# Deformable-convolution stage of a four-layer MetaFormer kernel: tap-group products added up by accumulating DMAs, four product buffers, reductions three halves later

## The chip, the cores and the metric

One core of a Trainium2 chip runs one program. The metric is the device time of one execution in microseconds. The five engines run their own instruction queues and meet only at semaphores: TensorE (PE), VectorE (DVE), ScalarE (ACT), GpSimd (POOL) and SyncE (SP, here only loads and stores). PEld is TensorE's weight load.

## The reference, cut to what matters

A batch of 8 images, 32 channels, 16x16 pixels in float32, passes four layers. Each is a convolution-like mixer and a mixture-of-experts block, both with a normalisation before and a residual after. The change lies in the mixer of layer 2, a deformable convolution (DCNv4) that is applied twice in a row:

```
value  = t @ Wv + bv                       # 4 groups of 8 channels
om     = t @ Wom + bom                     # offsets and masks: 9 taps x 4 groups x 3 per pixel
loc    = pixel + tap + offset              # a real position per pixel, tap and group
out    = sum over taps( bilinear(value, loc) * mask ) @ Wo
x      = batchnorm(out), relu after the first of the two passes
```

The kernel writes the bilinear sample as two hat functions, max(0, 1 - |dx|) over the columns of the image and max(0, 1 - |dy|) times the mask over its rows. The column part is a matrix product, the row part an elementwise product, and the sum runs over rows and taps together.

## The kernel before, in words

One application is a *turn* (`deform(turn)` on each engine); there are two. A turn has 8 images `b`, each in two *halves* of 128 pixels, so 16 halves `h`. A pixel has a partition. The 9 taps of a half are three groups `t` of three taps. For each group:

- PE, `products`: 6 matrix products (hats of the columns `HX` against the values `VB`) into one of two pairs of PSUM banks, alternating by group. The group waits until the one before last has been read (`prod_used`).
- DVE, `sample` (L852): multiplies the 864 PSUM columns by the row hats `HY` and writes them to `PRD`, at the place of group `t` in the buffer of the half. Column order is point group (2), channel (16), tap and row (27).

The sum over 3 groups x 27 columns is then split. POOL's `pairs` (L294) adds group 0 to group 1 (864 columns). POOL's `last` (L301) adds the first half (432 columns) of group 2 to that sum. DVE's `sums` (L864) reduces 27 columns to one for the first 16 channels, and 2 x 27 to one for the other 16, whose group 2 is still apart, into `SMT`. `PRD` has two buffers, one for each half of an image, so `sample` waits for the `sums` and `last` of two halves before.

DVE's order, fixed in the code (L887 to L900), is: two samples, the sums of the half before, the third sample. After b = 1 five instructions (`points`) prepare images 4 to 7. POOL's order is: row distances of the next image (`rows_off`, 2 instructions), `pairs`, `last` of half 0, masks of the next image (`masked`, 2 instructions), `pairs`, `last` of half 1. PE's order interleaves, per image, six groups of products with one transpose of the next image's points (`turn_points`) and three `spread`s (3 matrix products each, which copy the column positions to 128 partitions). ACT turns the spread positions into hats: `points_out` (L499), then three times `hats` (three Abs at L515, one Relu at L518), and `rows_hat` (L505, L507) for the rows.

After the 16 halves PE runs 22 filler products (`keep_warm`), waits for all sums (`smp_ready`), and a chain of short steps on all engines does the projection and the batch normalisation before the next turn or the next layer.

`wb` holds the weights of the layers before; its 6137 columns are not read any more when a turn starts.

Of the kernel before, what the change touches and what calls it, by code (L numbers as in the profile page):

```python
# [11 lines left out]
B, C, HH, WW = 8, 32, 16, 16  # L12
NPIX = HH * WW
P = 128
B4 = P // C
# [6 lines left out]
G, CG, K9 = 4, 8, 9  # L22
NA, NR = 2, 9
GP = G // 2
PADW = HH + 2
KG = K9 * G
COLS = 2 * CG * NR
HYN = KG * NR
TRIO = 3 * GP * COLS
PRN = 3 * TRIO  # L30
HXN = K9 * NPIX
LXW = 96
BIG = 1e30
# [54 lines left out]
def metaformer(nc, x_in, cst_in, wa_in, wb_in, wc_in, wd_in, out):  # L88
    fp32 = mybir.dt.float32
    ALU, ACT, AX = mybir.AluOpType, mybir.ActivationFunctionType, mybir.AxisListType  # L90

    with ExitStack() as ctx:
        widths = {}

        def sb(name, cols, parts=P):
            t = ctx.enter_context(nc.sbuf_tensor(name, [parts, cols], fp32))
            widths[name] = cols
            return t

        def view(t, col, dims, p0=0, n=P):  # L100

            if isinstance(t, tuple):
                t, first = t
                col = first + col
            if isinstance(t, Bank):
                t, col = psum, t.at + col
            w = t.shape[1]
            return bass.AP(t, p0 * w + col, [[w, n]] + [list(d) for d in dims])

        sem = lambda name: ctx.enter_context(nc.semaphore(name))  # L110
# [4 lines left out]
        cst, wa, wb, wc, wd = sb("cst", NCST), sb("wa", NWA), sb("wb", NWB), sb("wc", NWC), sb("wd", NWD)  # L115
# [33 lines left out]

        HX, LXT, XW = (RINGS, 0), (RINGS, 2 * HXN), (RINGS, 2 * HXN + NPIX)  # L150
        HY = sb("HY", 2 * 2 * HYN)
        PRD = sb("PRD", 2 * PRN)
        SMT = sb("SMT", F)
        KC, YV = (PRD, 0), (PRD, F)

        psum = ctx.enter_context(nc.psum_tensor("bank", [P, 8 * 512], fp32))
# [60 lines left out]
        def pointed(turn, b):  # L217
# [3 lines left out]
        t_done, lxt_ready, sel_done, abs_done, hat_ready, dy_ready, hy_abs, hy_ready, hym_ready, prod_done, prod_used = (  # L221
            sem(n) for n in ("t_done", "lxt_ready", "sel_done", "abs_done", "hat_ready", "dy_ready", "hy_abs", "hy_ready",
                             "hym_ready", "prod_done", "prod_used"))
        paired = sem("paired")
        smp_ready, smp_turned, sc_ready, mean_done, mean_ready, sum_ready, sum_done, cen_ready, sq_ready, sq_done, bn_ready, dc_ready = (
            sem(n) for n in ("smp_ready", "smp_turned", "sc_ready", "mean_done", "mean_ready", "sum_ready", "sum_done", "cen_ready",
                             "sq_ready", "sq_done", "bn_ready", "dc_ready"))
# [5 lines left out]
        def after(eng, s, value):  # L233

            if not isinstance(value, int) or value > 0:
                eng.wait_ge(s, value)
# [20 lines left out]
        def _(pool):  # L257
# [33 lines left out]
                    ins = pool.tensor_tensor(hy, hy, by_point(MM, 2 * b + half), ALU.mult)  # L291
                ins.then_inc(hym_ready, 1)

            def pairs(turn, b, half):  # L294

                i = B * turn + b
                pool.wait_ge(prod_used, 6 * i + 3 * half + 2)
                first, second = (view(PRD, half * PRN + t * TRIO, [[1, TRIO]]) for t in range(2))
                pool.tensor_tensor(second, second, first, ALU.add).then_inc(paired, 1)  # L299

            def last(turn, b, half):  # L301

                i = B * turn + b
                pool.wait_ge(prod_used, 6 * i + 3 * half + 3)
                pool.wait_ge(paired, 4 * i + 2 * half + 1)
                second, third = (view(PRD, half * PRN + t * TRIO, [[1, TRIO // GP]]) for t in (1, 2))
                pool.tensor_tensor(second, second, third, ALU.add).then_inc(paired, 1)  # L307

            def top2(turn):
# [42 lines left out]
            for turn in range(2):  # L352
                rows_off(turn, 0)
                masked(turn, 0)
                for b in range(B):
                    if b + 1 < B:
                        rows_off(turn, b + 1)
                    pairs(turn, b, 0)
                    last(turn, b, 0)
                    if b + 1 < B:  # L360
                        masked(turn, b + 1)
                    pairs(turn, b, 1)
                    last(turn, b, 1)
            pool.wait_ge(prod_done, 2 * B * 6)
            pool.memset(view(VM, 0, [[1, HEADS * F]]), 0.0).then_inc(km_clear, 1)
            top2(1)
# [5 lines left out]
        def _(act):  # L372
# [136 lines left out]
            def hats(i, t):  # L509

                after(act, prod_done, 6 * (i - 1))
                hx = i % 2 * HXN + 3 * t * NPIX
                for quad in range(3):
# [79 lines left out]
        def _(dve):  # L593
# [257 lines left out]

            def sample(i, half, t):  # L852

                q = 6 * i + 3 * half + t
                dve.wait_ge(hym_ready, i + 1)
                after(dve, smp_ready, 2 * i + half - 1)
                after(dve, paired, 4 * i + 2 * half - 2)
                dve.wait_ge(prod_done, q + 1)
                dve.tensor_tensor(view(PRD, half * PRN + t * TRIO, [[3 * COLS, GP], [6 * NR, CG], [1, 6 * NR]]),  # L859
                                  view(bank[q % 2 * 2], 0, [[512, GP], [6 * NR, CG], [1, 6 * NR]]),  # L860
                                  view(HY, (i % 2 * 2 + half) * HYN + t * 3 * G * NR, [[6 * NR, GP], [0, CG], [1, 6 * NR]]),
                                  ALU.mult).then_inc(prod_used, 1)

            def sums(i, half):  # L864

                bh, b4 = divmod(i % B, B4)
                at = bh * NPIX + half * P + b4 * C
                dve.wait_ge(prod_used, 6 * i + 3 * half + 3)
                dve.wait_ge(paired, 4 * i + 2 * half + 2)
                dve.tensor_reduce(view(SMT, at, [[1, C // 2]]),  # L870
                                  view(PRD, half * PRN + TRIO, [[3 * NR, C // 2], [1, 3 * NR]]), AX.X, ALU.add)
                dve.tensor_reduce(view(SMT, at + C // 2, [[1, C // 2]]),  # L872
                                  view(PRD, half * PRN + TRIO + TRIO // GP, [[3 * NR, C // 2], [TRIO, 2], [1, 3 * NR]]), AX.XY,
                                  ALU.add).then_inc(smp_ready, 1)

            def deform(turn):
                offsets(turn, 0, 0)
                offsets(turn, 0, 1)
                points(0, 1)
                if turn == 0:  # L880
                    dve.wait_ge(vb_clear, 2)
                values(turn, 0)
                values(turn, 1)
                offsets(turn, 1, 0)
                offsets(turn, 1, 1)
                points(1, B4 - 1)
                for b in range(B):  # L887
                    i = B * turn + b
                    sample(i, 0, 0)
                    sample(i, 0, 1)  # L890
                    if b:
                        sums(i - 1, 1)
                    sample(i, 0, 2)
                    sample(i, 1, 0)
                    sample(i, 1, 1)
                    sums(i, 0)
                    if b == 1:
                        points(B4, B4)
                    sample(i, 1, 2)
                sums(B * turn + B - 1, 1)  # L900

                dve.wait_ge(sum_done, turn + 1)
                dve.tensor_copy(c1[:, 1:2], bank[2][:, 0:1]).then_inc(sum_ready, 1)
                dve.wait_ge(mean_done, turn + 1)
                dve.tensor_scalar(c1[:, 0:1], bank[3][:, 0:1], -1.0, None, ALU.mult).then_inc(mean_ready, 1)
                dve.wait_ge(sq_ready, turn + 1)
                dve.tensor_scalar(ACC[:, :], bank[1][:, :], c1[:, 0:1], None, ALU.add).then_inc(cen_ready, 1)
                dve.wait_ge(cen_ready, turn + 1)
                dve.wait_ge(sq_done, turn + 1)
                dve.tensor_scalar(c2[:, 2:3], bank[4][:, 0:1], 1e-5, None, ALU.add).then_inc(bnv_ready, 1)  # L910
                dve.wait_ge(bsd_ready, turn + 1)
                link(dve.reciprocal(c1[:, 3:4], c2[:, 1:2]))
                dve.tensor_tensor(c1[:, 2:3], c1[:, 3:4], wc[:, WC["gamma"]:WC["gamma"] + 1], ALU.mult).then_inc(bn_ready, 1)
                dve.wait_ge(bn_ready, turn + 1)
# [52 lines left out]
            for bh in range(NBH):  # L967
                for j in range(2):
                    at = (2 * bh + j) * P
# [15 lines left out]
        def _(pe):  # L985
# [240 lines left out]
            def products(turn, b, half, t):  # L1226
# [9 lines left out]
                for k3 in range(3):  # L1236
                    for gp in range(GP):
                        ins = pe.matmul(view(bank[q % 2 * 2 + gp], k3 * NR, [[3 * NR, 2 * CG], [1, NR]]),  # L1238
                                        view(HX, b % 2 * HXN + (3 * t + k3) * NPIX + half * P, [[1, P]], 64 * gp, 64),
                                        view(VB, b * COLS, [[NR, 2 * CG], [1, NR]], 64 * gp, 64),  # L1240
# [3 lines left out]
            def deform(turn, src):  # L1244
# [40 lines left out]
                pe.wait_ge(smp_ready, 16 * turn + 16)  # L1285
                turn4(bank[0], SMT, smp_turned)
                pe.wait_ge(sc_ready, turn + 1)
# [252 lines left out]
```

## Time and profile before

| | us |
|---|---|
| median of 3 runs (lowest, highest) | 507.6 (506.81, 508.44) |
| the profiled execution | 508.54 |
| span of its trace, first to last instruction | 506.7 |
| PE busy | 428.1 (84%) |
| DVE busy | 386.3 (76%) |
| ACT busy | 298.2 (59%) |
| POOL busy | 179.5 (35%) |

Busy time is the time in which the engine runs an instruction. The granted TensorE clock was 0.931 of full speed over the span. Positions in the text, such as 280.3 us, are counted from the span's start. The first turn's first sample is at 192.2 us and its last sum ends at 280.3 us; the second turn's last sum ends at 389.8 us.

### The profile page before, as it was taken

What the parts mean: (1) busy time and instruction counts of PE and PEld (TensorE: products, weight loads), DVE (VectorE), ACT (ScalarE), POOL (GpSimd) and SP (SyncE); (2) the same over time, 40 slices, a digit from 0 to 9 for tenths busy, and PEclk for the clock granted to TensorE, in tenths of its full rate; (3) what the DMA queues carried; (4) which work ended last, traced back from release to release, by engine and by line L of the source; (5) the groups of instructions that cost most, each with busy time, mean ns of one, the idle gap of its engine ahead of it and who ended that gap; (6) DMA issues with size and microseconds to landing.
All of it is one profiled execution on the core that took longest, in us unless ns stands there. A gap on an engine that the chain in (4) does not pass through costs nothing.

```text
span 506.7 us, 10694 instructions
## 1 busy us (share of the span) xinstructions
PE 428.1 (84%) x3942; PEld 294.2 (58%) x3942; DVE 386.3 (76%) x838; ACT 298.2 (59%) x634; POOL 179.5 (35%) x169
## 2 busy tenths in 40 slices
PE   6989889999988767878887879688878899699685
PEld 6868723333327645656566656566667888455474
DVE  4878899998956286789998565988996686899541
ACT  2743248888944248768880277677860323898440
POOL 5002470000000024769997045788985041000000
PEclk9999989999999598879999966988998999999995
DMA  8800000000000000000000000000000000000000
GB/s 329 352 1 1 1 0 2 1 0 1 1 0 1 1 2 1 2 2 0 3 1 1 1 2 1 1 1 1 2 3 0 1 1 1 1 2 2 1 1 21
DMA packets 1486, 9.51 MB, mean 19 GB/s; under 512 B 160, under 2 KB 928, under 8 KB 1056
## 3 DMA queue, kind: packets, MB, share of 16 engines
q1 hardware_dynamic: 1296, 8.81, 4.3%
q8 instruction: 31, 0.51, 0.4%
q14 instruction: 15, 0.12, 0.1%
q10 hardware_dynamic: 144, 0.07, 0.1%
HBM read 8.62 MB, written 0.26 MB: 18 GB/s over the span
## 4 chain that ended last, share of the span: by engine, by line
PE 53%; DVE 25%; ACT 13%; issue 6%; POOL 2%; DMA 0%; DVEq 0%; SPq 0%; POOLq 0%
PE bank L1238 13%; PE bank L1180 13%; PE bank L994 5%; PE bank L1223 4%; DVE SMT L872 4%; ACT RINGS L515 3%; DVE PRD L859 3%; ACT RINGS L566 3%; DVE RINGS L791 2%; PE bank L1345 2%; PE bank L1185 2%; DVE SMT L870 2%; PE bank L1325 2%; PE bank L1250 1%; POOL PR L314 1%
## 5 line engine op out<-in xcount | busy, mean ns | idle before, releaser
L1238 PE MATMUL bank<-VB,RINGS 64*128 64x144 f32 x1152 | 107.4, 330 | 25.2 <-DVE PRD L859 24.2
L859 DVE TENSOR_TENSOR PRD<-bank,HY 128x864 f32<-128x864 f32 x96 | 99.0, 1052 | 29.5 <-PE bank L1238 28.2
L1238 PEld LDWEIGHTS bank<-VB,RINGS 64*128 64x128 f32 x1152 | 88.4, 213 | 50.8 <-DVE PRD L859 23.6
L791 DVE TENSOR_SCALAR RINGS<-XP,wb 128x512 f32<-128x512 f32 x176 | 79.4, 527 | 7.9 <-PE bank L1180 6.6
L478 ACT ACTIVATE RINGS<-XP,wb 128x512 f32<-128x512 f32 x112 | 70.0, 714 | 17.0 <-PE bank L1180 16.9
L994 PE MATMUL bank<-cst 128*128 128x128 f32 x650 | 79.7, 283 | 0.0
L994 PEld LDWEIGHTS bank<-cst 128*128 128x128 f32 x650 | 78.3, 200 | 0.7 <-issue 0.3
L1180 PE MATMUL bank<-RINGS,cst 128*32 128x512 f32 x576 | 74.6, 600 | 3.5 <-DVE RINGS L791 3.4
L515 ACT ACTIVATE RINGS<-bank,cst 128x256 f32<-128x256 f32 x144 | 57.5, 469 | 26.4 <-PE bank L1223 26.4
L299 POOL TENSOR_TENSOR PRD<-PRD 128x864 f32<-128x864 f32 x32 | 64.7, 2022 | 17.6 <-DVE PRD L859 17.4
L282 POOL TENSOR_TENSOR HY<-OM,cst 128x324 f32<-128x324 f32 x32 | 23.3, 751 | 127.6 <-DVE LXA L841 127.6
L1180 PEld LDWEIGHTS bank<-RINGS,cst 128*32 128x32 f32 x576 | 22.9, 110 | 53.5 <-issue 26.6
L1223 PE MATMUL bank<-RINGS,cst 32*128 32x256 f32 x288 | 38.3, 475 | 10.8 <-ACT RINGS L515 6.7
L518 ACT ACTIVATE RINGS<-RINGS,cst 128x768 f32<-128x768 f32 x48 | 44.9, 936 | 1.6
L307 POOL TENSOR_TENSOR PRD<-PRD 128x432 f32<-128x432 f32 x32 | 35.3, 1103 | 16.7 <-DVE PRD L859 16.6
L384 ACT ACTIVATE sd<-var,cst 128x8 f32<-128x8 f32 x16 | 4.8, 301 | 50.4 <-DVE var L618 50.2
L314 POOL TENSOR_TENSOR PR<-PR 128x256 f32<-128x256 f32 x16 | 11.5, 729 | 63.7 <-DVE PR L703 63.7
L872 DVE TENSOR_REDUCE SMT<-PRD 128x16 f32<-128x864 f32 x32 | 33.4, 1043 | 0.0
L566 ACT ACTIVATE RINGS<-RINGS,nm 128x256 f32<-128x256 f32 x64 | 31.5, 496 | 1.3 <-DVE nm L945 1.3
L1223 PEld LDWEIGHTS bank<-RINGS,cst 32*128 32x128 f32 x288 | 16.7, 205 | 20.5 <-issue 10.8
L1345 PE MATMUL bank<-cst,RINGS 128*128 128x128 f32 x128 | 20.8, 286 | 7.5 <-ACT RINGS L566 7.1
L291 POOL TENSOR_TENSOR HY<-HY,OM 128x324 f32<-128x324 f32 x32 | 23.5, 756 | 8.2 <-ACT HY L507 8.2
(253 smaller groups left out, 544.0 us busy)
## 6 DMA issues: line engine op xcount, KB each, us to landing
wb<-in_wb SPq DMA_DIRECT2D x1, 3068.5 KB, 12.3
wd<-in_wd SPq DMA_DIRECT2D x1, 2729.5 KB, 20.8
wc<-in_wc SPq DMA_DIRECT2D x1, 1255.0 KB, 14.8
cst<-in_cst SPq DMA_DIRECT2D x1, 829.5 KB, 5.3
XC<-in_x SPq DMA_DIRECT2D x2, 128.0 KB, 2.4
out_y<-XC SPq DMA_DIRECT2D x2, 128.0 KB, 1.8
wa<-in_wa SPq DMA_DIRECT2D x1, 209.0 KB, 5.5
cst<-in_cst ACTq DMA_DIRECT2D x1, 66.0 KB, 2.6
```

Of the source, the lines that this page charges most:

```text
L299: pool.tensor_tensor(second, second, first, ALU.add).then_inc(paired, 1)
L478: act.activation(view(RINGS, slot, [[NPIX, NBH], [WW, HH], [1, WW]]), view(XP, tap // 3 * PADW + tap % 3, [[PADW * PADW, NBH], [PADW, HH], ...
L515: act.activation(view(HX, hx + quad * NPIX, [[1, NPIX]]), bank[4 + quad][:, 0:NPIX], ACT.Abs, bias=cv("mx", 1)).then_inc(abs_done, 1)
L518: act.activation(view(HX, hx, [[1, 3 * NPIX]]), view(HX, hx, [[1, 3 * NPIX]]), ACT.Relu, scale=-1.0, bias=cv("one", 1)).then_inc(hat_ready, 1)
L566: ins = act.activation(view(SM3, at, [[1, 256]]), view(SM3, at, [[1, 256]]), ACT.Exp, scale=-1.0, bias=nm[:, u:u + 1], accum_out=rs[:, u:u ...
L791: dve.tensor_scalar(view(RINGS, (k % DRING) * F, [[NPIX, NBH], [WW, HH], [1, WW]]), view(XP, tap // 3 * PADW + tap % 3, [[PADW * PADW, NBH ...
L859: dve.tensor_tensor(view(PRD, half * PRN + t * TRIO, [[3 * COLS, GP], [6 * NR, CG], [1, 6 * NR]]), view(bank[q % 2 * 2], 0, [[512, GP], [6 ...
L872: dve.tensor_reduce(view(SMT, at + C // 2, [[1, C // 2]]), view(PRD, half * PRN + TRIO + TRIO // GP, [[3 * NR, C // 2], [TRIO, 2], [1, 3 * ...
L994: pe.matmul(bk[:, 0:P], ident, ident, start=True, stop=True)
L1180: pe.matmul(bank[2][32 * j:32 * j + 32, :], cv(rep, 32, 28 - 4 * i), RINGS[:, slot:slot + F], start=(i == 0 and tap == TAPS[0]), stop=(i = ...
L1223: pe.matmul(bank[4 + quad][:, 0:NPIX], cv("select", P, t * P, 32 * quad, 32), view(LXT, 0, [[1, NPIX]], 32 * quad, 32), start=True, stop=T ...
L1238: ins = pe.matmul(view(bank[q % 2 * 2 + gp], k3 * NR, [[3 * NR, 2 * CG], [1, NR]]), view(HX, b % 2 * HXN + (3 * t + k3) * NPIX + half * P, ...
```

## The change

For the first 14 halves of each turn (`BY_DMA = 14`) both additions leave POOL's arithmetic. POOL issues two DMAs instead, each from `PRD` to `PRD` with an addition at the destination: `add_first` adds group 0 onto group 1, `add_third` adds group 2 onto group 1 when the first has landed. Both move 128 partitions x 864 columns. `sums` is then one reduction of 864 columns. Halves 14 and 15 keep the old way. Four product buffers are used: two in `PRD`, two in `wb`. `sums` of a half stand three halves later in DVE's order.

```
+SLOTS = 4
+BEHIND = 3
+BY_DMA = 14
...
+        def prd(h):
+            s = h % SLOTS
+            return (PRD, s * PRN) if s < 2 else (wb, (s - 2) * PRN)
...
+        first_added, third_added = ([sem(f"{n}_added{s}") for s in range(SLOTS)] for n in ("first", "third"))
+        def added(h):
+            return 16 * sum(g % SLOTS == h % SLOTS and g % (2 * B) < BY_DMA for g in range(h + 1))
...
+            def add_first(h):
+                pool.wait_ge(prod_used, 3 * h + 2)
+                first, second = (view(prd(h), t * TRIO, [[1, TRIO]]) for t in range(2))
+                pool.dma_start(second, first, accum_op=ALU.add).then_inc(first_added[h % SLOTS], 16)
+            def add_third(h):
+                pool.wait_ge(prod_used, 3 * h + 3)
+                pool.wait_ge(first_added[h % SLOTS], added(h))
+                second, third = (view(prd(h), t * TRIO, [[1, TRIO]]) for t in (1, 2))
+                pool.dma_start(second, third, accum_op=ALU.add).then_inc(third_added[h % SLOTS], 16)
...
             for turn in range(2):
                 rows_off(turn, 0)
                 masked(turn, 0)
-                for b in range(B):
-                    if b + 1 < B:
+                for n in range(2 * B):
+                    h, (b, half) = 2 * B * turn + n, divmod(n, 2)
+                    if half == 0 and b + 1 < B:
                         rows_off(turn, b + 1)
-                    pairs(turn, b, 0)
-                    last(turn, b, 0)
-                    if b + 1 < B:
+                    if 0 < n <= BY_DMA:
+                        add_third(h - 1)
+                    if n < BY_DMA:
+                        add_first(h)
+                    else:
+                        pairs(turn, h)
+                        last(turn, h)
+                    if half == 0 and b + 1 < B:
                         masked(turn, b + 1)
-                    pairs(turn, b, 1)
-                    last(turn, b, 1)
...
             def sample(i, half, t):
-                q = 6 * i + 3 * half + t
+                q, h = 6 * i + 3 * half + t, 2 * i + half
                 dve.wait_ge(hym_ready, i + 1)
-                after(dve, smp_ready, 2 * i + half - 1)
-                after(dve, paired, 4 * i + 2 * half - 2)
+                after(dve, smp_ready, h - SLOTS + 1)
...
+                if n < BY_DMA:
+                    dve.wait_ge(third_added[h % SLOTS], added(h))
+                    dve.tensor_reduce(view(SMT, at, [[1, C]]), view(prd(h), TRIO, [[3 * NR, C], [1, 3 * NR]]), AX.X,
+                                      ALU.add).then_inc(smp_ready, 1)
+                    return
...
                     sample(i, half, 0)
                     sample(i, half, 1)
+                    if n >= BEHIND:
+                        sums(turn, h - BEHIND)
+                    if b == half == 1:
+                        points(B4, B4)
                     sample(i, half, 2)
+                for n in range(2 * B - BEHIND, 2 * B):
+                    sums(turn, 2 * B * turn + n)
```

## Rows read from the trace of the kernel before

**Rows 1.** Chain that ended last, the page's shares of the span by line.

```profile
PE bank L1238 13%; PE bank L1180 13%; PE bank L994 5%; PE bank L1223 4%; DVE SMT L872 4%; ACT RINGS L515 3%; DVE PRD L859 3%; ACT RINGS L566 3%; DVE RINGS L791 2%; PE bank L1345 2%; PE bank L1185 2%; DVE SMT L870 2%; PE bank L1325 2%; PE bank L1250 1%; POOL PR L314 1%
```

**Rows 2.** Groups of instructions: total busy us, mean ns, idle before and releaser.

```profile
L859 DVE TENSOR_TENSOR PRD<-bank,HY 128x864 f32<-128x864 f32 x96 | 99.0, 1052 | 29.5 <-PE bank L1238 28.2
L299 POOL TENSOR_TENSOR PRD<-PRD 128x864 f32<-128x864 f32 x32 | 64.7, 2022 | 17.6 <-DVE PRD L859 17.4
L307 POOL TENSOR_TENSOR PRD<-PRD 128x432 f32<-128x432 f32 x32 | 35.3, 1103 | 16.7 <-DVE PRD L859 16.6
```

**Rows 3.** Timeline of DVE, one image of the first turn: start, duration, [idle before].

```profile
257.35 2.01 DVE L859 TENSOR_TENSOR PRD<-bank,HY 128x864 f32<-128x864 f32 x2
259.76 1.06 DVE L859 TENSOR_TENSOR PRD<-bank,HY 128x864 f32<-128x864 f32 x1 [0.40 <-PE bank L1238]
260.74 0.59 DVE L870 TENSOR_REDUCE SMT<-PRD 128x16 f32<-128x432 f32 x1
261.25 1.04 DVE L872 TENSOR_REDUCE SMT<-PRD 128x16 f32<-128x864 f32 x1
262.21 2.01 DVE L859 TENSOR_TENSOR PRD<-bank,HY 128x864 f32<-128x864 f32 x2
...
266.90 2.01 DVE L859 TENSOR_TENSOR PRD<-bank,HY 128x864 f32<-128x864 f32 x2
```

**Rows 4.** Windows: busy PE, PEld, DVE, ACT, POOL; clock, DMA share, GB/s.

```profile
250.00:260.00 10.00, 8.43 (x102) 6.31 (x102) 9.15 (x11) 8.57 (x17) 9.45 (x10) 1.00 0.01 2
300.00:310.00 10.00, 9.65 (x58) 6.45 (x60) 4.93 (x6) 6.71 (x13) 5.21 (x5) 0.50 0.01 2
```

**Rows 5.** Timeline of ACT, the work for one image.

```profile
257.56 0.36 ACT L499 ACTIVATE RINGS<-bank 96x256 f32<-96x256 f32 x1
258.77 1.21 ACT L515 ACTIVATE RINGS<-bank,cst 128x256 f32<-128x256 f32 x3 [0.84 <-PE bank L1223]
260.00 0.94 ACT L518 ACTIVATE RINGS<-RINGS,cst 128x768 f32<-128x768 f32 x1
261.03 0.74 ACT L505 ACTIVATE HY<-HY 128x648 f32<-128x648 f32 x1
261.81 0.84 ACT L507 ACTIVATE HY<-HY,cst 128x648 f32<-128x648 f32 x1
```

**Rows 6.** Timeline of POOL: the pair sums of halves 0, 4 and 13 of both turns.

```profile
195.83 2.01 POOL L299 TENSOR_TENSOR PRD<-PRD 128x864 f32<-128x864 f32 x1 [2.61 <-DVE PRD L859]
...
222.49 2.02 POOL L299 TENSOR_TENSOR PRD<-PRD 128x864 f32<-128x864 f32 x1 [0.64 <-DVE PRD L859]
...
265.82 2.02 POOL L299 TENSOR_TENSOR PRD<-PRD 128x864 f32<-128x864 f32 x1
...
328.94 2.02 POOL L299 TENSOR_TENSOR PRD<-PRD 128x864 f32<-128x864 f32 x1
...
374.64 2.02 POOL L299 TENSOR_TENSOR PRD<-PRD 128x864 f32<-128x864 f32 x1
```

**Rows 7.** The page's DMA lines: queue's packets, MB and share of 16 engines; issues, KB, us to landing.

```profile
q1 hardware_dynamic: 1296, 8.81, 4.3%
...
XC<-in_x SPq DMA_DIRECT2D x2, 128.0 KB, 2.4
out_y<-XC SPq DMA_DIRECT2D x2, 128.0 KB, 1.8
```

**Rows 8.** Timeline of SP: one load's issue.

```profile
1.66 0.42 SPq L244 DMA_DIRECT2D cst<-in_cst  x1
```

**Rows 9.** Timeline of DVE at the end of turn 1, then of turn 2.

```profile
276.38 1.05 DVE L859 TENSOR_TENSOR PRD<-bank,HY 128x864 f32<-128x864 f32 x1
278.71 0.60 DVE L870 TENSOR_REDUCE SMT<-PRD 128x16 f32<-128x432 f32 x1 [1.28 <-POOL PRD L307]
279.23 1.04 DVE L872 TENSOR_REDUCE SMT<-PRD 128x16 f32<-128x864 f32 x1
...
388.78 1.04 DVE L872 TENSOR_REDUCE SMT<-PRD 128x16 f32<-128x864 f32 x1
```

**Rows 10.** Timeline of DVE, half 2 of turn 1: a sample that waits, its sums.

```profile
208.34 1.06 DVE L859 TENSOR_TENSOR PRD<-bank,HY 128x864 f32<-128x864 f32 x1 [1.43 <-PE bank L1238]
209.32 0.59 DVE L870 TENSOR_REDUCE SMT<-PRD 128x16 f32<-128x432 f32 x1
209.83 1.04 DVE L872 TENSOR_REDUCE SMT<-PRD 128x16 f32<-128x864 f32 x1
```

**Rows 11.** Timeline of PE at the end of turn 2: filler products, then the transposes of the sums.

```profile
384.72 5.36 PE L994 MATMUL bank<-cst 128*128 128x128 f32 x44
389.92 0.62 PE L988 MATMUL bank<-cst,SMT 128*128 128x128 f32 x4
```

**Rows 12.** Timeline of PE: one group of products at either clock level.

```profile
190.42 1.71 PE L1238 MATMUL bank<-VB,RINGS 64*128 64x144 f32 x12 [0.17 <-ACT RINGS L518]
...
255.33 1.01 PE L1238 MATMUL bank<-VB,RINGS 64*128 64x144 f32 x12
```

More of the change, by code:

```diff
@@ L292, in masked, with pairs, last @@
                 ins.then_inc(hym_ready, 1)
[L294 to L298, printed above, removed]
-                pool.tensor_tensor(second, second, first, ALU.add).then_inc(paired, 1)
[L301 to L306, printed above, removed]
+            def add_first(h):
[7 more added lines that the diff above has]
+                pool.dma_start(second, third, accum_op=ALU.add).then_inc(third_added[h % SLOTS], 16)
+            def pairs(turn, h):
+                pool.wait_ge(prod_used, 3 * h + 2)
+                first, second = (view(prd(h), t * TRIO, [[1, TRIO]]) for t in range(2))
+                pool.tensor_tensor(second, second, first, ALU.add).then_inc(paired, 1)
+            def last(turn, h):
+                pool.wait_ge(prod_used, 3 * h + 3)
+                pool.wait_ge(paired, 4 * turn + 2 * (h % (2 * B) - BY_DMA) + 1)
+                second, third = (view(prd(h), t * TRIO, [[1, TRIO // GP]]) for t in (1, 2))
                 pool.tensor_tensor(second, second, third, ALU.add).then_inc(paired, 1)
@@ L852, in sample @@
             def sample(i, half, t):
-                q = 6 * i + 3 * half + t
+                q, h = 6 * i + 3 * half + t, 2 * i + half
                 dve.wait_ge(hym_ready, i + 1)
-                after(dve, smp_ready, 2 * i + half - 1)
-                after(dve, paired, 4 * i + 2 * half - 2)
+                after(dve, smp_ready, h - SLOTS + 1)
                 dve.wait_ge(prod_done, q + 1)
-                dve.tensor_tensor(view(PRD, half * PRN + t * TRIO, [[3 * COLS, GP], [6 * NR, CG], [1, 6 * NR]]),
+                dve.tensor_tensor(view(prd(h), t * TRIO, [[3 * COLS, GP], [6 * NR, CG], [1, 6 * NR]]),
                                   view(bank[q % 2 * 2], 0, [[512, GP], [6 * NR, CG], [1, 6 * NR]]),
@@ L862, in sample, with sums @@
                                   ALU.mult).then_inc(prod_used, 1)
[L864 to L871, printed above, removed]
+            def sums(turn, h):
+                n = h % (2 * B)
+                bh, b4 = divmod(n // 2, B4)
+                at = bh * NPIX + n % 2 * P + b4 * C
+                if n < BY_DMA:
[3 more added lines that the diff above has]
+                    return
+                dve.wait_ge(prod_used, 3 * h + 3)
+                dve.wait_ge(paired, 4 * turn + 2 * (n - BY_DMA) + 2)
+                dve.tensor_reduce(view(SMT, at, [[1, C // 2]]), view(prd(h), TRIO, [[3 * NR, C // 2], [1, 3 * NR]]), AX.X,
+                                  ALU.add)
                 dve.tensor_reduce(view(SMT, at + C // 2, [[1, C // 2]]),
-                                  view(PRD, half * PRN + TRIO + TRIO // GP, [[3 * NR, C // 2], [TRIO, 2], [1, 3 * NR]]), AX.XY,
+                                  view(prd(h), TRIO + TRIO // GP, [[3 * NR, C // 2], [TRIO, 2], [1, 3 * NR]]), AX.XY,
                                   ALU.add).then_inc(smp_ready, 1)
@@ L886, in deform @@
                 points(1, B4 - 1)
-                for b in range(B):
+                for n in range(2 * B):
+                    h, (b, half) = 2 * B * turn + n, divmod(n, 2)
                     i = B * turn + b
[L889 to L897, printed above, removed]
+                    sample(i, half, 0)
+                    sample(i, half, 1)
+                    if n >= BEHIND:
+                        sums(turn, h - BEHIND)
+                    if b == half == 1:
                         points(B4, B4)
-                    sample(i, 1, 2)
-                sums(B * turn + B - 1, 1)
+                    sample(i, half, 2)
+                for n in range(2 * B - BEHIND, 2 * B):
+                    sums(turn, 2 * B * turn + n)
                 dve.wait_ge(sum_done, turn + 1)
```

## The prediction, written before the change was run

> **What bounds the kernel now.** I read the chain that ended last first, to see whether the edited instructions are on it at all. They are: the two reductions (L872, L870) hold 4% and 2% of the span, the samples (L859) 3%; POOL's additions are not among its lines [rows 1]. The groups show POOL's two additions at 2022 and 1103 ns, 3.1 us a half, and the sample at 1052 ns, which waits only for PE [rows 2]. The timeline says what an image costs in the steady part: from 257.35 to 266.90 is 9.55 us for six samples and two pairs of reductions, with DVE idle 0.40 us before one sample of a half [rows 3]. In 10 us DVE is busy 9.15, POOL 9.45, ACT 8.57 and PE 8.43 [rows 4]. So DVE sets the pace, POOL is nearly as full but is only waited for at a turn's end, and ACT and PE are about a tenth behind. [...]
>
> **The change part by part.** *DVE's reductions.* The pair costs 262.21 - 260.74 = 1.47 us in line, of which 0.51 (261.25 - 260.74) is the 432-column one and 0.96 the 864-column one [rows 3]. One 864-column reduction remains: 0.51 us less in each of 28 halves, 14.3 us of DVE work. That is the most the removal can give.
>
> *How much of it arrives.* ACT is next. Its work for an image is one L499 (0.36), three times L515 (1.21) and L518 (0.94), L505 (0.74) and L507 (0.84), 8.39 us, and after L499 it must sit 0.84 us until PE has spread the new points [rows 5]: 9.2 us an image. So 9.55 falls to 9.2, not to 8.5: 0.35 us for each of five steady images, 1.8 us a turn. Image 7 has no successor to prepare and gets its full 1.0. Half 2, whose reductions (1.5 us) stood behind a sample that had waited for PE 1.43 us [rows 10], loses them from the chain because sums come three halves later: 1.5 at most. About 4.3 us a turn.
>
> *The tail.* Before, DVE's last sample ends at 276.38 + 1.05 = 277.43 and the last reduction at 279.23 + 1.04 = 280.27, 2.8 us later, 1.28 of it waiting for POOL [rows 9]. Now three sums follow the last sample: 0.96 + 1.47 + 1.47 = 3.9 us. Cost 1.1 us a turn if nothing is late. PE's 22 fillers lie beside it; in turn 2 they ran until 384.72 + 5.36 = 390.1 with the last sum at 389.8 [rows 9, 11], so up to 0.3 us of a longer tail is covered there.
>
> *Buffers.* Four buffers remove the waits for `sums` and `last` of two halves before. Those waits hardly show (28.2 of 29.5 us of the sample's idle time is for PE [rows 2]): worth 1.3 us at most, priced at nothing.
>
> *The new transfers.* This decides. There are 56, each 128 x 864 x 4 = 442 KB at the destination, and each must fetch both terms of the sum. Nothing like them is in the trace, so I bound them. All loads and stores of the hardware queue moved 8.81 MB in 4.3% of 16 x 506.7 engine-us [rows 7], which is 25.3 GB/s an engine, 404 GB/s for 16. One pass of 442 KB is then 1.09 us (low end), two reads in a row 2.19 us. I take 2.19, because the operation has two inputs where those rows have one; a rate below that of a copy would be worse still, and I keep 3.1 us as the far end, what the two additions cost POOL [rows 2]. The fixed part: a 128 KB store lands in 1.8 us and a load in 2.4 [rows 7]; less 0.32 us of data that is 1.5 to 2.1, middle 1.8. An issue occupies the queue 0.42 us on SP [rows 8]; on POOL it can cost more, and anything up to the 3.1 us a half of arithmetic that it replaces leaves POOL no fuller than now.
>
> *The wait it adds.* POOL holds `add_third(h)` until the first transfer of h has landed, and `add_first(h+1)` stands behind it. The third's data is then in flight ahead of the first's, so in a saturated state the loop from one `add_third` to the next is fixed part + both data times: 1.8 + 2 x 2.19 = **6.2 us a half**. It is self-sustaining once fixed + two data times exceed DVE's half, 9.2 / 2 = 4.6 us. Its ends are 1.5 + 2 x 1.09 = 3.7 (no loop, all fits) and 2.1 + 6.2 = 8.3. Also behind the wait are `rows_off` and `masked` of the next image; they have two halves of slack. DVE meets it at `sums(h-3)`, with the third sample behind it, and PE behind that.
>
> *The sum.* Half 4's pair sum is at 222.49 in turn 1; two halves of early gain put it at about 220.6, where the loop from 195.83 also puts it (4 x 6.2 = 24.8) [rows 6]. First landing adds 1.8 + 2.19 = 4.0; nine more loops of 6.17 bring `add_third(13)` to 224.6 + 55.5 = 280.1. It lands 4.0 later, 284.1, and sums of 13 and 14 end at 286.5. POOL's `pairs(14)`, `last(14)` and `pairs(15)`, `last(15)` run 280.1 + 2 x 3.1 = 286.3 to about 286.8 with the issue, and the last sums end at 288.3: 8.0 us later than 280.3. In turn 2 half 4 is at 328.94, 327 with the early gain [rows 6]; 327 + 4.0 + 55.5 + 8.2 = 394.7 against 389.8 and PE's 390.1: 4.6 us later. Together +12.6 us. The profiled execution took 508.54, so 521.1; the median of the runs is 0.9 lower than that execution, so **about 520 us**.
>
> [...]
>
> **The rivals.** *A: everything fits.* If a transfer is not slowed by its second read (1.09 us) or the fixed part is small, the first lands before the next half's third sample and nothing waits. Then a turn gains 4.3 - 1.1 = 3.2 us, 6.4 in all: 508.54 - 6.4 - 0.9 = 501 us. With ACT's wait shorter than I priced it the gain rises towards 14.3 - 2.2 = 12 us, 495. For it: DMA queues are idle now, share 0.01 [rows 4]. The early halves are slow, 222.49 - 195.83 is 6.7 us a half [rows 6], and give the loop no trouble. Against: two transfers a half at one read each already fill half of the time. *B: the loop lands at the break-even.* Nine loops between half 4 and half 13 now have (265.82 - 222.49) / 9 = 4.8 us each [rows 6]; with early gain and tail the times of before come back at a loop of 5.3 us in turn 1 and 5.6 in turn 2. Between 5.4 and 5.5: 507.6. *C: slower accumulation.* At the far end of 8.3 us a loop it is (8.3 - 6.2) x 18 = 38 us more, 558; with 7.2, 538. POOL taking several us to issue ends here too. The side turns at 5.45 us a loop: below it is A's side, above it mine.
>
> A lower granted clock is a follower, not a rival: at the half clock a group of products takes 1.71 instead of 1.01 us [rows 12], and PE still fits in 6.2 us a half. It may add 1 to 2 us behind each turn's end.
>
> **How the numbers follow.** The loop at 5.6 to 6.9 us (511 to 535 us): 0.43. C, above that: 0.12. B: 0.07. A and all loops under 5.4: 0.38, most of it at 496 to 505. So slower by over 0.3% 0.55, within 0.3% (1.5 us, about what a measurement of this kernel can tell from nothing) 0.07, faster 0.38. The range must reach A's main body and C's beginning: 496 to 540, leaving out some 0.06 below and 0.11 above.
>
> **What would show it.** In the profile of the changed kernel: the time from issue to landing of the PRD transfers, over 4.5 us if I am right, under 4 if A holds; the distance between POOL's issues of `add_third` in halves 4 to 13, 6.2 or 4.6 us; DVE's idle time before the 864-column reduction, released by a DMA, over 1 us a half or none; one reduction of 0.96 us where two stood; three sums in a row at a turn's end; busy DMA engines near full in the steady part. ACT's image at 9.2 us and idle behind L499 is the test of A's ceiling. I am wrong if the transfers land in time for the next third sample, or if the reads of both terms overlap.

## The result, and the profile after

| | before | changed |
|---|---|---|
| median of 4 runs, us | 507.21 (506.37 to 508.44) | 565.11 (563.52 to 570.66) |
| span of the profiled execution, us | 506.7 | 563.7 |
| granted TensorE clock over the span | 0.931 | 0.87 |
| DVE / POOL busy, us | 386.3 / 179.5 | 373.0 / 143.3 |

The ratio is 1.1159 (95% interval 1.1079 to 1.1239): 58 us slower. The direction was forecast, the size was not: 520 us, range 496 to 540.

The chain that ended last has a new first place. The page's line by source, to be held against [rows 1]:

```profile
DMA PRD<-PRD 12%; PE bank L1213 11%; DMA wb<-wb 10%; PE bank L1271 5%; PE bank L1027 3%; ACT RINGS L596 3%; DVE RINGS L821 2%; PE bank L1256 2%; ACT RINGS L545 2%; PE bank L1378 2%; PE bank L1358 2%; PE bank L1218 2%; POOL wb L326 1%; POOL PRD L320 1%; PE bank L1283 1%
```

The transfers hold 22% of the chain, DVE's reductions no longer stand among its first places. In order of time, from 230 us on (start, duration, what; in the changed kernel L313 is `add_first`, L320 `add_third`):

```profile
231.35 5.98 DMA PRD<-PRD
...
237.37 0.49 issue
237.86 0.58 POOL PRD L320
238.45 5.96 DMA wb<-wb
...
244.45 0.49 issue
244.94 0.43 POOL wb L320
```

Nothing else is in it. From one `add_third` to the next are 244.94 - 237.86 = 7.08 us: 0.59 to the issue of the next first, 5.96 to its landing, 0.53 until POOL issues again. I call this the loop. The timeline of POOL shows the same loop with what lies beside it:

```profile
230.76 0.88 POOL L320 DMA_DIRECT2D PRD<-PRD  x1 [4.15 <-DMA PRD<-PRD]
231.35 1.18 POOL L313 DMA_DIRECT2D PRD<-PRD  x1
231.91 2.09 POOL L297 TENSOR_TENSOR HY<-OM,cst 128x324 f32<-128x324 f32 x2
237.86 0.88 POOL L320 DMA_DIRECT2D PRD<-PRD  x1 [3.86 <-DMA PRD<-PRD]
238.45 1.17 POOL L313 DMA_DIRECT2D wb<-wb  x1
...
294.97 0.85 POOL L320 DMA_DIRECT2D PRD<-PRD  x1 [5.66 <-DMA PRD<-PRD]
```

The waits in brackets are idle time of POOL ahead of the instruction. 22 of the 28 `add_third` of both turns waited so for a landing, 86.6 us in all. Four more waits (15.1 us) the profile puts down to a sample of DVE, but they too ended 0.5 us after the landing of their first: one was issued at 209.55 us and landed 6.0 later, and its `add_third` follows at 216.05. So 26 of 28 waited for a landing, all but the first of each turn. The time from issue to landing, of `add_first` and then of `add_third` (56 transfers in all), and the queue's line on the page (packets, MB, share of 16 engines):

```profile
DMA to landing us min/median/max: 4.2/6.0/7.3
DMA to landing us min/median/max: 4.2/4.2/4.8
q0 software_dynamic: 8064, 24.78, 23.8%
```

A third, alone on the queue when it starts, lands in 4.2 us. A first issued 0.6 us behind it lands in 6.0. The queue's share gives 0.238 x 16 x 563.7 / (56 x 16) = 2.40 us of data time a transfer, which is the time that its packets took on each of the 16 engines. DVE, which was busy 9.15 of 10 us [rows 4], is busy 7.19 in the same window of time, and the DMA share is 0.58:

```profile
250.00:260.00 10.00, 7.83 (x90) 5.78 (x92) 7.19 (x8) 6.34 (x13) 4.04 (x6) 1.00 0.58 107
```

The end of turn 1, timeline of DVE, answers to [rows 9]:

```profile
292.79 1.05 DVE L888 TENSOR_TENSOR wb<-bank,HY 128x864 f32<-128x864 f32 x1
299.15 1.05 DVE L900 TENSOR_REDUCE SMT<-PRD 128x32 f32<-128x864 f32 x1 [5.32 <-DMA PRD<-PRD]
300.12 0.59 DVE L905 TENSOR_REDUCE SMT<-wb 128x16 f32<-128x432 f32 x1
...
303.27 1.04 DVE L907 TENSOR_REDUCE SMT<-wb 128x16 f32<-128x864 f32 x1
...
312.70 0.16 DVE L946 TENSOR_TENSOR c<-c,wc 128x1 f32<-128x1 f32 x1
```

The last sum ends at 304.31 instead of 280.27 us. From there to L946, the end of the batch-norm factors, are 8.4 us; before it were 5.4.

### The profile page after: what moved, and what is told of

Read it like the earlier page. It is cut to its first block, busy times and chain, and to the rows that moved or that the text cites. A ratio compares the mean times of both kernels' runs of the same rounds, so it can differ in the third digit from the quotient of the medians.

```text
span 563.7 us, 10548 instructions
## 1 busy us (share of the span) xinstructions
PE 454.1 (81%) x3942; PEld 314.0 (56%) x3942; DVE 373.0 (66%) x810; ACT 298.7 (53%) x634; POOL 143.3 (25%) x169
## 3 DMA queue, kind: packets, MB, share of 16 engines
q0 software_dynamic: 8064, 24.78, 23.8%
## 4 chain that ended last, share of the span: by engine, by line
PE 39%; DMA 22%; DVE 17%; ACT 10%; POOL 6%; issue 5%; DVEq 0%; POOLq 0%; SPq 0%
DMA PRD<-PRD 12%; PE bank L1213 11%; DMA wb<-wb 10%; PE bank L1271 5%; PE bank L1027 3%; ACT RINGS L596 3%; DVE RINGS L821 2%; PE bank L1256 2%; ACT RINGS L545 2%; PE bank L1378 2%; PE bank L1358 2%; PE bank L1218 2%; POOL wb L326 1%; POOL PRD L320 1%; PE bank L1283 1%
## 5 line engine op out<-in xcount | busy, mean ns | idle before, releaser
L1271 PE MATMUL bank<-VB,RINGS 64*128 64x144 f32 x1152 | 120.1, 360 | 10.3 <-DVE wb L888 7.3
L1271 PEld LDWEIGHTS bank<-VB,RINGS 64*128 64x128 f32 x1152 | 100.0, 239 | 38.9 <-issue 22.8
L888 DVE TENSOR_TENSOR PRD<-bank,HY 128x864 f32<-128x864 f32 x48 | 50.1, 1054 | 40.8 <-PE bank L1271 40.6
L1256 PE MATMUL bank<-RINGS,cst 32*128 32x256 f32 x288 | 41.9, 514 | 41.0 <-ACT RINGS L545 38.4
L888 DVE TENSOR_TENSOR wb<-bank,HY 128x864 f32<-128x864 f32 x48 | 49.8, 1054 | 32.2 <-PE bank L1271 27.2
L297 POOL TENSOR_TENSOR HY<-OM,cst 128x324 f32<-128x324 f32 x32 | 29.0, 1108 | 134.0 <-DVE LXA L871 130.1
L306 POOL TENSOR_TENSOR HY<-HY,OM 128x324 f32<-128x324 f32 x32 | 30.2, 1171 | 12.9 <-ACT HY L537 12.8
L900 DVE TENSOR_REDUCE SMT<-PRD 128x32 f32<-128x864 f32 x16 | 16.8, 1048 | 19.9 <-DMA PRD<-PRD 19.9
L535 ACT ACTIVATE HY<-HY 128x648 f32<-128x648 f32 x16 | 11.8, 737 | 33.0 <-POOL HY L297 33.0
L320 POOL DMA_DIRECT2D PRD<-PRD x16 | 13.9, 870 | 55.2 <-DMA PRD<-PRD 47.5
## 6 DMA issues: line engine op xcount, KB each, us to landing
wb<-in_wb SPq DMA_DIRECT2D x1, 3068.5 KB, 12.3
```

Source lines behind the costliest of these rows:

```text
L297: ins = pool.tensor_tensor(by_trio(HY, (b % 2 * 2 + half) * HYN), by_point(LY, 2 * b + half), view(cst, CST["yg"], [[0, 3], [0, 3 * G], [1 ...
L888: dve.tensor_tensor(view(prd(h), t * TRIO, [[3 * COLS, GP], [6 * NR, CG], [1, 6 * NR]]), view(bank[q % 2 * 2], 0, [[512, GP], [6 * NR, CG] ...
L1256: pe.matmul(bank[4 + quad][:, 0:NPIX], cv("select", P, t * P, 32 * quad, 32), view(LXT, 0, [[1, NPIX]], 32 * quad, 32), start=True, stop=T ...
```

## The experiments

All start from the changed kernel. Ratios are to the kernel before.

**One issue moved.** Nothing is added or left out:

```
-                    if 0 < n <= BY_DMA:
-                        add_third(h - 1)
                     if n < BY_DMA:
                         add_first(h)
+                    if 0 < n <= BY_DMA:
+                        add_third(h - 1)
```

> The changed kernel with one thing moved: GpSimd issues add_first(h) before add_third(h-1), not behind it, so no issue stands behind the wait for a landing of the same half. Theory 1 (the cost is the loop issue, landing, next issue of 7.1 us a half, made by GpSimd's order): the loop opens, a half takes what VectorE or the two data times take, 4.6 to 4.9 us, and the kernel takes 504 to 516 us, thirds still landing in 4 to 7 us. Theory 2 (the transfers are too slow for the stage, whatever their order): two of them fill a half of about 7 us as before, 555 to 565 us. Theory 3 (buffers and late sums disturb PE and ScalarE): unchanged, 560 us or more.

Measured: 500.53 us, ratio 0.9874 (0.9774 to 0.9974). Once more, with this expectation:

> The kernel with add_first(h) issued ahead of add_third(h-1), once more, on the same chip as the two beside it and in five rounds: 499 to 502 us, 1.0 to 1.5% less than the kernel before. If the first result was a chip's luck, 504 us or more.

502.08 us, ratio 0.9896 (0.9857 to 0.9934). Theory 1 holds, 2 and 3 fall: two swapped issues turn 58 us of loss into some 5 to 6 us of gain. That is 2 to 4 us better than theory 1's range, which began at 504 us. The transfers are not faster for it. Landing of `add_first` and `add_third`, the queue, and a window of the first of the two runs:

```profile
DMA to landing us min/median/max: 4.2/5.6/6.7
DMA to landing us min/median/max: 4.2/6.5/7.6
q0 software_dynamic: 8064, 24.78, 26.9%
240.00:250.00 10.00, 8.77 (x107) 6.57 (x104) 8.67 (x9) 8.99 (x18) 7.51 (x10) 1.00 1.04 191
```

The data time is 0.269 x 498.5 / 56 = 2.39 us as before, and the thirds land later than in the changed kernel; but now each has more than a half in which to do it. A DMA share of 1.04 means that the engines are hardly ever without a packet of these transfers. Two data times, 4.8 us, pass in a half of 4.5 us, so the packets of two transfers overlap a little. They do not set the pace: a form below with half as many transfers has the same one. Images come every 9.05 us (255.57 - 246.52 in DVE's timeline), where the changed kernel needs 14.2:

```profile
246.52 2.01 DVE L888 TENSOR_TENSOR wb<-bank,HY 128x864 f32<-128x864 f32 x2
248.77 1.06 DVE L888 TENSOR_TENSOR wb<-bank,HY 128x864 f32<-128x864 f32 x1 [0.24 <-PE bank L1271]
250.32 1.05 DVE L900 TENSOR_REDUCE SMT<-PRD 128x32 f32<-128x864 f32 x1 [0.49 <-DMA PRD<-PRD]
...
255.57 2.01 DVE L888 TENSOR_TENSOR PRD<-bank,HY 128x864 f32<-128x864 f32 x2
```

**No transfers, the rest of the change kept.** `BY_DMA = 0`, with the counts of `paired` set to match.

> The changed kernel with BY_DMA = 0: four buffers and sums three halves later stay, all additions go back to GpSimd and the two reductions to VectorE. Theories 1 and 2 (the transfers are the cost): 505 to 511 us, the tail of three sums (4.4 us after the last sample instead of 2.8) against up to 1.5 us saved at the start of a turn. Theory 3 (the new order and buffers are the cost): well over 530 us.

513.19 us, ratio 1.0069 (1.0017 to 1.0121). Theory 3 falls again. The result is some 2 us above the range: a turn's last sum ends 2.1 us later than before (three sums of 1.47 us in a row), and the batch-norm stage behind it takes 6.9 instead of 5.4 us, which I had not priced.

**Copies instead of additions.**

```
-                pool.dma_start(second, first, accum_op=ALU.add)...
+                pool.dma_start(second, first)...        (both transfers)
```

> The changed kernel with its 56 transfers as plain copies: the additions of groups 0 and 2 are left out of the result. If the second read makes the data time (2.4 us of engine time a transfer), a copy needs 1.1 to 1.2 us of it, a third lands in 3.0 instead of 4.2 us, the loop falls from 7.1 to about 4.7 us and the kernel takes 505 to 516 us. If the addition costs nothing beside a copy, landing stays 4.2 and 6.0 us and the time 560 to 570 us.

502.98 us in one run, 2 us below the range. Landing of first and third, and the queue:

```profile
DMA to landing us min/median/max: 2.9/3.5/5.2
DMA to landing us min/median/max: 2.7/2.8/4.2
q0 software_dynamic: 4480, 24.78, 12.5%
```

Data time 0.125 x 501.2 / 56 = 1.12 us for the same 24.78 MB, in 4480 instead of 8064 packets. The addition costs 2.1 times the engine time of the copy. In turn 1, from 237.70 to 260.58 us, five loops take 4.58 us each, about the half of 4.5 us that the reordered kernel needs anyway.

**Half the columns.** `[[1, TRIO]]` becomes `[[1, TRIO // 2]]` in both transfers.

> The changed kernel with transfers of 432 instead of 864 columns: the other half of the columns of groups 0 and 2 is left out of the sum. If the data time goes with bytes, it halves to 1.2 us, a third lands in about 3.0 us, the loop is 4.7 us and the kernel takes 505 to 516 us. If it goes with rows (128 of them, as before), landing stays 4.2 and 6.0 us and the time 560 us or more.

512.54 us in one run. The third lands in 3.1 us, the queue's share gives 0.145 x 510.7 / 56 = 1.32 us. POOL's timeline has the loops from half 4 to half 13:

```profile
DMA to landing us min/median/max: 3.1/3.1/4.7
q0 software_dynamic: 8064, 12.39, 14.5%
...
224.49 0.88 POOL L320 DMA_DIRECT2D PRD<-PRD  x1 [2.93 <-DMA PRD<-PRD]
229.44 0.88 POOL L320 DMA_DIRECT2D PRD<-PRD  x1 [1.70 <-DMA PRD<-PRD]
...
271.02 0.85 POOL L320 DMA_DIRECT2D PRD<-PRD  x1 [3.17 <-DVE wb L888]
```

Data time goes with bytes for the most part (1.32 against 2.40), not with rows. Both runs shorten the loop in the unchanged order of issues. The copies bring it down to the length of a half. With half the columns it is 4.9 us at best and 5.2 on average ((271.02 - 224.49) / 9), still longer than a half, and the kernel is the slower of the two.

**More filler products.** `FILL_TAIL = 60` instead of 22.

> The changed kernel with 60 instead of 22 filler products at a turn's end: 38 more at 0.235 us each are 8.9 us, as long as PE now stands idle for the last sums (9.0 us). Theory: of the 57 us between the two spans, 24 to 25 us a turn are the loop of transfers and the tail, and 3 us a turn behind it are PE's clock, fallen in the idle time (from the last sum to the batch-norm factors 8.4 us instead of 5.4). Then this takes 5 to 7 us off: 557 to 561 us. Rival: the 3 us a turn are waits that have nothing to do with the clock: no change, 563 us or more.

562.3 us, ratio 1.1136 (1.1064 to 1.1208), span 559.0 instead of 563.7. That is 1 us above the range, and the ratio's interval overlaps that of the changed kernel, so the total alone decides nothing. The stage does: in turn 1 PE ran 13.7 us of fillers up to 304.2, and from the last sum (305.15) to L946 are 5.4 us again, as before the change.

```profile
304.11 1.04 DVE L907 TENSOR_REDUCE SMT<-wb 128x16 f32<-128x864 f32 x1
...
310.56 0.16 DVE L946 TENSOR_TENSOR c<-c,wc 128x1 f32<-128x1 f32 x1
```

The windows from the last sum to L946 show the granted clock (1.00, 0.55, 1.00, 0.75, the number behind the busy times) in turn 1 before, in turn 1 of the changed kernel, and in both turns of this run:

```profile
280.27:285.68 5.41, 4.58 (x33) 3.87 (x34) 1.39 (x6) 1.76 (x6) 0.00 (x0) 1.00 0.00 0
304.31:312.70 8.39, 7.56 (x32) 6.13 (x33) 1.39 (x6) 1.76 (x6) 0.00 (x0) 0.55 0.00 0
305.15:310.56 5.41, 4.57 (x33) 3.86 (x34) 1.39 (x6) 1.76 (x6) 0.00 (x0) 1.00 0.01 3
439.15:446.07 6.92, 6.08 (x32) 4.82 (x33) 1.39 (x6) 1.76 (x6) 0.08 (x1) 0.75 0.00 0
```

Only PE's busy time differs. So the 3.0 us that this stage had grown by were PE's clock (0.55 instead of 1.00) after 9.0 us of idling; the fillers gave all of it back in turn 1 and half of it in turn 2, where PE stood idle for 1.4 us again before the last sum.

**Transfers in seven halves of a turn.** `BY_DMA = 7`, issue order as in the change.

> The changed kernel, issue order as in the change, with the transfers for the first 7 halves of a turn only. Theory (7.1 us for every half with transfers, from the first one on): half 6's add_third is issued at about 244.7 us in turn 1 where its last addition was at about 234.7 before, so a turn is 10 us longer at that point, plus 1 to 2 us of tail and clock behind it; 22 to 25 us in all, 529 to 533 us. Rival (my earlier sum: the slow first halves of a turn hide the loop, only halves from 4 on pay): 3 loops a turn of 2.3 us, 7 us a turn, 518 to 523 us. Rival (the cost sits at a turn's end): 550 us or more.

538.31 us, ratio 1.0633 (1.0573 to 1.0693). Half 6's `add_third` is issued at 244.56 us, as theory 1 said, so the loop costs from the first half on, and the rival that only halves from 4 on pay is refuted. But the whole is 5 us above my range. It is not lost in turn 1, whose last sum ends at 292.6 us, 12.3 later than before and near the forecast. The spans of the two profiles differ by 28.0 us: those 12.3, then 10.7 in turn 2, 2.5 in the stage behind it and 2.4 in all that follows, and for the last two I had counted almost nothing. ACT's timeline shows another thing that I had not counted:

```profile
250.17 0.74 ACT L535 ACTIVATE HY<-HY 128x648 f32<-128x648 f32 x1 [5.05 <-POOL HY L297]
```

`rows_off` (L297) for image 5 stood behind the last `add_third` and POOL's own additions; ACT waited 5 us for it, with the hats of the next image behind, and DVE then sat 4.9 us before a sample at 255.89. What this wait costs is not shown, since no run moved `rows_off` alone. It is not the missing 5 us: from half 6's `add_third` to the last sum of turn 1 are 48.0 us, against 45.6 from half 6's last addition before the change, and 2.1 us of the difference stand in the run without transfers too.

**Fillers for the reordered kernel, and two other forms.**

> The kernel with add_first(h) issued ahead of add_third(h-1) and 29 instead of 22 filler products: PE idles 1.2 us before the last sum there, and the stage behind it took 6.9 instead of 5.4 us. If that is the clock, 1 to 3 us less than the same kernel with 22: 497.5 to 499.5 us. If not, no change or up to 1.5 us more where the fillers end late.

502.89 us, 0.9907 (0.9863 to 0.9951): inconclusive against 0.9896 for 22 fillers on the same chip; the batch-norm stage kept its 6.9 us, so these seven did nothing there.

One transfer a half: `pairs(turn, h)` in place of `add_first(h)`, `add_third` waits for `paired`, `SLOTS = 3`, `BEHIND = 2`.

> GpSimd adds group 0 to group 1 itself in all halves, one transfer a half adds group 2 (864 columns) onto the sum; three buffers, sums two halves later. VectorE has the one reduction of 864 columns as in the change. If the pace of the kernel with two transfers is set by ScalarE (8.99 of 10 us busy), the image stays at 9.05 us, transfers land 4.2 us after issue, the tail is one sum shorter: 497 to 501 us. If GpSimd becomes the bound (2.0 + 0.7 for masks and offsets + about 1.2 for an issue, 3.9 to 4.7 us a half), the image takes up to 9.5 us and the kernel 502 to 507 us.

500.05 us, 0.989 (0.9837 to 0.9943), as fast as with two transfers. POOL is busy 9.48 of 10 us in a window and ACT 8.99, and the transfers land in 4.2 to 4.3 us at the median: ScalarE's pace holds, POOL's does not bind yet.

```profile
240.00:250.00 10.00, 8.78 (x112) 6.73 (x110) 8.07 (x9) 8.99 (x18) 9.48 (x10) 1.00 0.48 88
```

Reordered, 13 halves by transfer, 29 fillers:

> The kernel with add_first(h) issued ahead of add_third(h-1), with the transfers for 13 instead of 14 halves of a turn and 29 fillers. Theory: in the 14-halves form GpSimd starts the pair sum of half 14 only after add_third(13), 3.7 us late, and the turn's tail after the last sample is 5.7 us; one half more on GpSimd costs VectorE 0.5 us and shortens the tail by about 1.2 us, so 0.5 to 1.5 us a turn less: 497 to 501 us. Rival: the tail is set by the length of GpSimd's additions (3.1 us a half, now three halves in a row): no change or 1 us more, 500 to 504 us.

499.03 us, 0.9857 (0.9809 to 0.9904), the best of all. Its last sum of turn 1 ends at 274.61 instead of 275.82 us, with no wait for a transfer or for POOL among the last sums, and the stage behind takes 5.4 us. Its interval overlaps those of the other two forms, and two things were changed at once: the fillers alone had brought nothing, but no run has the thirteen halves alone.

```profile
269.16 1.05 DVE L888 TENSOR_TENSOR wb<-bank,HY 128x864 f32<-128x864 f32 x1
270.12 0.59 DVE L905 TENSOR_REDUCE SMT<-PRD 128x16 f32<-128x432 f32 x1
...
273.57 1.04 DVE L907 TENSOR_REDUCE SMT<-wb 128x16 f32<-128x864 f32 x1
```

## Why the prediction was wrong in size

**The mechanism was right.** A first landing behind a third in POOL's queue, `add_third` waiting for it and `add_first` behind the wait: the chain consists of it, and the swap of two issues removes it. The spans grew by 57.0 us where the sum had 12.6, so 44.4 us are to be found.

**The loop, 7.1 us instead of 6.2: the step that failed most.** The term fixed part + two data times is 0.59 + 5.97 = 6.56 measured, 6.17 priced. The fixed part was 4.2 - 2.4 = 1.8 us, as taken from [rows 7]. The data time was 2.40, not 2.19 us: I doubled the copy's 1.09 us (the copies measured 1.12), and the addition costs 2.1 times, not twice. The other 0.5 us is a term that I left out: from landing to the next issue POOL takes 0.53 us. Over the nine loops from half 4 to 13 (64.2 and 64.7 us against 55.5) that is 17.8 us in both turns.

**The first four halves of a turn** I did not count as loops that grow. I put half 4's `add_third` at 224.6 us, from half 4's place before the change; four loops of 6.2 us from half 0 led to the same place, so the same short loop stood behind it, and a longer one would have moved it. Counted from the turns' starts it stood 7.5 and 9.1 us later than I had it, 16.6 us:

```profile
195.28 1.01 POOL L313 DMA_DIRECT2D PRD<-PRD  x1 [3.41 <-DVE PRD L888]
200.44 1.46 POOL L306 TENSOR_TENSOR HY<-HY,OM 128x324 f32<-128x324 f32 x2 [4.14 <-ACT HY L537]
201.85 0.86 POOL L320 DMA_DIRECT2D PRD<-PRD  x1
```

Of these, 9.1 us are again the loop: the four halves after the first `add_third` took 28.9 and 30.7 us (7.2 each in turn 1, 230.76 - 201.85) where the sum leaves 24.8 and 25.8. A second term is missing: `masked` of the next image (L306), which waits for ACT, stands between the first `add_first` and the first `add_third`, which follows after 6.6 and 7.3 us instead of 4.0. That is 5.9 us. The last 1.7 us are a later first issue. That these halves gave the loop no trouble was wrong: the 6.7 us a half that I read there [rows 6] is less than the loop, and with the loop open they take only 5.8 (the four distances from half 0 to 4 in the reordered kernel, 195.40 to 218.78). `BY_DMA = 7` shows it. So the loop's length makes 17.8 + 9.1 = 26.9 of the 44.4 us.

**The tail** was 9.3 and 9.0 us from the last `add_third` against 8.2: 1.9 us. With the 12.6 us forecast that makes 12.6 + 17.8 + 16.6 + 1.9 = 48.9 us, where the two stages (from the first `rows_off` to the last sum, 95.2 and 99.4 us before, 120.6 and 123.3 after) grew by 49.3.

**The clock** I called a follower of 1 to 2 us a turn and left out of the sum. It was 3.0 us a turn, 6 us. The rest of the 57.0 us lies outside: 3.1 us more from the second turn's L946 to the end, where the granted clock is 0.91 instead of 0.94, and 1.3 us less before the first turn. No run shows the cause of these two.

**Slack of `rows_off`.** Two halves of slack was too much credit: in the changed kernel ACT waited 33.0 us for L297 in all. This is also how the wait reaches DVE for the most part. I had it arrive at `sums`, over 1 us a half; there DVE waited 19.9 us for transfers, 0.7 a half. It waited 67.8 us for PE before samples (28.2 before the change [rows 2]), PE in turn for ACT's hats, and those stand behind `rows_off`. What this path would cost by itself no run shows; the loop is on the chain that ended last, and this path is not.

**Rivals.** A was not what the change did, but its time is what the swapped order gives: 501 us forecast, 500.5 and 502.1 measured. Its conditions do not hold there (data time 2.39 us, a first lands in 5.6); what it had right is the bound that remains, ScalarE, with 9.05 us an image against 9.2 forecast. C gave 538 us for a loop of 7.2 us: it too multiplied the excess by nine loops a turn and not by thirteen. B's break-even of 5.3 to 5.6 us is not settled. Half columns came nearest, with 5.2 us and 512.5 us in one run, no gain on the kernel before; the copies lie below it, with 4.6 us and 503.0.

## What to carry to other kernels

A transfer whose landing its own issuing engine must await puts everything behind the wait on that latency (here 7.1 us a half, 4.5 with the two issues swapped): issue the next independent transfer ahead of the wait, not behind it, and count the loop as issue, queue ahead, data, landing, wake-up. When such a loop exceeded the stage's period it held from its first round (7.2 us each in the first four halves of turn 1), so count all its rounds, not only the steady ones. Work given to another engine pays only until the next engine's pace, here ScalarE's (9.05 us an image), and idle time of PE can cost more in the stage after: at a granted clock of 0.55 behind 9.0 us of idling in turn 1 that stage took 3.0 us longer, at 0.75 behind 1.2 us (one issue moved, turn 1) 1.5 us, and at 1.00 behind 1.0 us (60 fillers, turn 1) nothing.

## What the runs showed of the hardware

- An accumulating transfer of 442 KB within SBUF took 2.40 us of each of the 16 DMA engines and landed 4.2 us after its issue, a copy 1.12 and 2.8 us; at half the size, with the addition, 1.32 and 3.1 us. Landing less data time is 1.8, 1.7 and 1.8 us.
- Its issue costs POOL 0.9 us, as its row of 0.87 says, but in part later. The next instruction starts 0.56 to 0.59 us behind it, and two `rows_off` or `masked` behind two issues take 2.10 instead of 1.46 us. From the issue at 230.76 to the end of the two `rows_off` at 234.00 are 3.24 us; less 1.46 this leaves 0.89 an issue. A copy's issue row is 0.54 us.
- Two transfers queued behind each other in the changed kernel overlapped only in their fixed parts: 4.2 us for the first, 2.4 us more for the second.
- One TENSOR_SCALAR of DVE, of `points`, ended only behind the tensor instruction of POOL that ran when it started, though the code has it wait for no semaphore of POOL's. In turn 1: before the change (L837, with POOL's instruction beside it), in the changed kernel (L867, POOL waits for a landing), and in the run without transfers, again with POOL's:

```profile
215.49 1.11 DVE L837 TENSOR_SCALAR BX<-OM 128x288 f32<-128x288 f32 x1
214.41 2.02 POOL L299 TENSOR_TENSOR PRD<-PRD 128x864 f32<-128x864 f32 x1
```

```profile
213.05 0.30 DVE L867 TENSOR_SCALAR BX<-OM 128x288 f32<-128x288 f32 x1
```

```profile
215.13 2.15 DVE L867 TENSOR_SCALAR BX<-OM 128x288 f32<-128x288 f32 x1
215.11 2.01 POOL L326 TENSOR_TENSOR wb<-wb 128x864 f32<-128x864 f32 x1
```

  It ended 0.17 and 0.16 us after POOL's, at 216.60 and 217.28. With one transfer a half it did so in both turns (1.22 and 1.50 us). In turn 2 of the run without transfers it started 0.09 us ahead of POOL's and took 0.30 us.
